# Attention loop of a two-layer megakernel: the transposes move into the PSUM rings of the scores, three banks read by VectorE and four read by ScalarE

## What is computed

```python
def _L1_attn_ref(x, Wqkv, bqkv, Wo, bo):     # 32 query heads, 8 key/value heads, head size 8
    qkv = jnp.einsum('bsd,df->bsf', x, Wqkv) + bqkv
    ...
    k = jnp.repeat(k, N_REP, axis=2)
    v = jnp.repeat(v, N_REP, axis=2)
    scores = jnp.einsum('bqhd,bkhd->bhqk', q, k) / np.sqrt(HEAD_DIM)
    attn = jax.nn.softmax(scores, axis=-1)
    out = jnp.einsum('bhqk,bkhd->bqhd', attn, v).reshape(bsz, seqlen, D_MODEL)
    return jnp.einsum('bsd,de->bse', out, Wo) + bo
```

## Time and profile before

| what | value |
|---|---|
| runs | 674.20, 677.84, 679.25 us; median 677.84 |
| the profiled execution, its own time | 674.86 us |
| span of its trace | 673.0 us |
| mean granted TensorE clock | 0.977 of full speed |
| attention loop in the trace | some 361 to 567 us |
| 13 "o" transposes of steps c = 12 to 60 | 398.57 to 535.13 us |

### The profile page before, as it was taken

The page is one execution under the profiler, slowest core; times in us unless marked ns, Lnnn a source line. Parts: engine busy times, 40 slices in busy tenths (PEclk is TensorE's granted clock), DMA queues, the critical chain, the costliest instruction groups (busy, mean ns, idle before and its releaser), DMA issues.

```text
span 673.0 us, 11796 instructions
## 1 busy us (share of the span) xinstructions
PE 617.5 (92%) x4298; PEld 408.7 (61%) x4298; DVE 400.7 (60%) x929; ACT 326.0 (48%) x645; POOL 213.5 (32%) x312
## 2 busy tenths in 40 slices
PE   3999999999999989799989899999999999979990
PEld 2887887887888775466566444444444446546660
DVE  4526605733751586333387979989899955633336
ACT  4523423432432324233326488888888885413322
POOL 5870651381082164523422121201010101421331
PEclk9999999999999999899979999999999999989995
DMA  6000200200199994314199991000000000031213
GB/s 218 33 1 33 95 1 32 93 1 1 68 265 278 77 270 138 96 39 135 50 310 333 282 118 3 1 2 1 2 1 2 1 2 1 25 99 44 80 56 125
DMA packets 69000, 57.40 MB, mean 85 GB/s; under 512 B 21520, under 2 KB 64400, under 8 KB 68944
## 3 DMA queue, kind: packets, MB, share of 16 engines
q1 hardware_dynamic: 66736, 50.60, 32.3%
q0 software_dynamic: 2208, 6.05, 2.5%
HBM read 30.78 MB, written 25.85 MB: 84 GB/s over the span
## 4 chain that ended last, share of the span: by engine, by line
PE 76%; DVE 7%; ACT 6%; DMA 4%; POOL 2%; issue 2%; another core or an unknown queue 1%; SPq 0%; ACTq 0%; POOLq 0%; DVEq 0%
PE psum L1604 9%; PE psum L303 9%; PE psum L1574 8%; PE psum L304 8%; PE psum L305 8%; PE psum L1289 8%; PE psum L1318 5%; PE psum L1560 4%; ACT pr L1473 3%; PE psum L1213 2%; DVE stat L666 2%; PE psum L1532 2%; PE psum L1199 1%; PE psum L1589 1%; PE psum L1206 1%
## 5 line engine op out<-in xcount | busy, mean ns | idle before, releaser
L1710 DVE TENSOR_REDUCE mx<-psum 128x1 f32<-128x512 f32 x256 | 158.7, 682 | 20.2 <-PE psum L1574 19.4
L1473 ACT ACTIVATE pr<-psum 128x512 f32<-128x512 f32 x256 | 138.8, 598 | 27.6 <-PE psum L1589 26.8
L1574 PE MATMUL psum<-kT,qT 32*128 32x512 f32 x256 | 78.5, 497 | 2.7 <-DVE mx L1710 1.6
L1604 PE MATMUL psum<-pr,vals 128*32 128x256 f32 x1024 | 78.9, 395 | 0.0
L1589 PE MATMUL psum<-qT,kT 32*128 32x512 f32 x256 | 66.5, 496 | 0.0
L1574 PEld LDWEIGHTS psum<-kT,qT 32*128 32x128 f32 x256 | 33.9, 182 | 47.2 <-issue 22.5
L1289 PE MATMUL psum<-w_gu,xgT 128*128 x120 | 57.5, 602 | 0.0
L624 POOL DMA_INDIRECT routed_y<-yr,xg x30 | 28.9, 962 | 84.3 <-DVE yr L876 83.7
L1514 POOL CAST mp<-mx 128x16 bf16<-128x16 f32 x16 | 3.2, 198 | 154.3 <-DVE mx L1710 154.3
L1046 ACT ACTIVATE sg<-psum,xg 128x256 f32<-128x256 f32 x30 | 14.2, 474 | 63.1 <-PE psum L1289 59.1
L867 DVE SCALAR_TENSOR_TENSOR h<-psum,xg,sg 128x256 f32<-128x256 f32 x30 | 14.5, 484 | 50.8 <-ACT sg L1046 50.8
(11 more groups left out here) (214 smaller groups left out, 1401.5 us busy)
## 6 DMA issues: line engine op xcount, KB each, us to landing
sorted_x<-zeros SPq DMA_DIRECT2D x2, 9088.0 KB, 41.7
w_gu<-in_L_ffn_gate_w SPq DMA_DIRECT2D x16, 256.0 KB, 6.3
w_gu<-in_L_ffn_up_w SPq DMA_DIRECT2D x16, 256.0 KB, 6.4
w_d<-in_L_ffn_down_w SPq DMA_DIRECT2D x16, 256.0 KB, 6.4
xg<-sorted_x SPq DMA_DIRECT2D x30, 129.0 KB, 2.2
wk_f<-in_L_attn_Wk SPq DMA_DIRECT2D x4, 512.0 KB, 5.2
wq_f<-in_L_attn_Wq SPq DMA_DIRECT2D x4, 512.0 KB, 5.9
wv_f<-in_L_attn_Wv SPq DMA_DIRECT2D x4, 512.0 KB, 3.6
```

The lines of the kernel that those rows point to most:

```text
L1473: nc.scalar.activation(pr[d % 3][:, j], s2_bank(d, j), ACT.Exp, scale=SCALE).then_inc(exp_ready, 1)
L1574: mm(s1_bank(c, j), qT1[n % 2][rows, t * P:(t + 1) * P], kT[n // GH][rows, :], start=True, stop=True).then_inc(s1_made, 1)
L1604: last = mm(ps[AV_BANK][j * VW:(j + 1) * VW, cols], vals[:, n // NKV * TB + kc, n % NKV // GH * GH + j, :], pr[d % 3][:, j, cols], start=( ...
L1710: v.tensor_reduce(mx[n % 2][:, t, j:j + 1], s1_bank(c, j), AX.X, ALU.max, negate=True).then_inc(max_read, 1)
```

## The change

The bank of a tile is no longer fixed by its kind. Two lists are written out ahead of the loop. FOR_DVE holds what VectorE reads, in the order in which TensorE makes it: the four `scores1` tiles of a step, and behind them an "o" transpose, for the steps that have one while c < 64; they take turns in banks 0, 1, 2. FOR_ACT holds what ScalarE reads: the `scores2` tiles with the "q1", "q2" and "k" transposes between the second and the third, and the last three "o" (n = 13 to 15, at c = 64, 68, 72); they take turns in banks 3, 4, 5, 7. Whatever it is, an item waits until the item three (four) places ahead in its list has been read (`wait_bank`).

In TensorE's list the "o" transpose moves from between the two halves of the scores to behind both, ahead of the two `weigh` halves. `turn_att` now waits for 13 outputs in place of 8, because banks 0 and 1 are shared with outputs; `keep_warm`'s dummy matmuls at the end use a spare bank. VectorE, ScalarE and GpSimd keep their lists of instructions; only banks change there.

```diff
-        RING = 3
+        DVE_BANKS, ACT_BANKS = (0, 1, 2), (3, 4, 5, 7)
...
+        LATE_O = (STEPS - 12) // TB
+        FOR_DVE, FOR_ACT = [], []
+        for c_ in range(END):
+            new = [x_ for x_ in turns_at(c_)]
+            if c_ < STEPS:
+                FOR_DVE += [("s1", c_ * GH + j) for j in range(GH)]
+                FOR_DVE += [x_ for x_ in new if x_[0] == "o"]
+            if c_ >= LAG:
+                S2 = [("s2", s2_no(c_ - LAG, j)) for j in HEADS2] if c_ < STEPS + LAG else []
+                FOR_ACT += S2[:2] + [x_ for x_ in new if x_[0] != "o"] + S2[2:]
+                FOR_ACT += [x_ for x_ in new if x_[0] == "o" and x_[1] >= LATE_O]
...
+        def wait_bank(pe, item):
+
+            ring, banks = (FOR_DVE, DVE_BANKS) if item in FOR_DVE else (FOR_ACT, ACT_BANKS)
+            at_ = ring.index(item) - len(banks)
+            if at_ < 0:
+                return
+            kind, n = ring[at_]
+            if kind == "s1":
+                pe.wait_ge(max_read, n + 1)
+            elif kind == "s2":
+                pe.wait_ge(exp_ready, n + 1)
+            else:
+                wait_read(pe, ring[at_])
...
             def turn(what):
                 n = TURNS.index(what)
-                if n >= 2:
+                if what in FOR_DVE or what in FOR_ACT:
+                    wait_bank(pe, what)
+                elif n >= 2:
                     wait_read(pe, TURNS[n - 1])
...
                 for j in (2 * i, 2 * i + 1):
-                    k = c * GH + j
-                    if k >= RING:
-                        pe.wait_ge(max_read, k - RING + 1)
+                    wait_bank(pe, ("s1", c * GH + j))
...
                 for what in turns_at(c):
-                    if what == ("o", NG - 1):
-                        keep_warm(2, 3)
-                    turn(what)
+                    if what[0] != "o":
+                        turn(what)
                 if c < STEPS:
                     scores1(c, 1)
...
+                for what in turns_at(c):
+                    if what[0] == "o":
+                        if what[1] == NG - 1:
+                            keep_warm(2, SPARE)
+                        turn(what)
                 if 0 <= d - 2 < STEPS:
                     if (d - 2) % TB == 0:
                         weigh(d - 2, 0)
```

More of the change, by code:

```diff
@@ L1360, in build @@
         QKV_AT = 3
-        RING = 3
+        DVE_BANKS, ACT_BANKS = (0, 1, 2), (3, 4, 5, 7)
         HEADS2 = (2, 3, 0, 1)
         AV_BANK, TURN_BANK = 6, 7
-        def s1_bank(c, j):
-            return ps[(c * GH + j) % RING]
         def s2_no(d, j):
             return d * GH + HEADS2.index(j)
-        def s2_bank(d, j):
-            return ps[RING + s2_no(d, j) % RING]
         def turns_at(c):
@@ L1396, in turn_no, with bank_no, s1_bank, s2_bank @@
             return TURNS.index(what) + 1
-        def turn_bank(n):
-            return ps[AV_BANK] if n == 0 else ps[TURN_BANK]
+        LATE_O = (STEPS - 12) // TB
[9 more added lines that the diff above has]
+                FOR_ACT += [x_ for x_ in new if x_[0] == "o" and x_[1] >= LATE_O]
+        SPARE = [i for i in ACT_BANKS if all(ACT_BANKS[FOR_ACT.index(("o", n)) % len(ACT_BANKS)] != i
+                                             for n in range(LATE_O, NG))][0]
+        def bank_no(item):
+            if item in FOR_DVE:
+                return DVE_BANKS[FOR_DVE.index(item) % len(DVE_BANKS)]
+            if item in FOR_ACT:
+                return ACT_BANKS[FOR_ACT.index(item) % len(ACT_BANKS)]
+            return AV_BANK if item == FIRST[0] else TURN_BANK
+        def s1_bank(c, j):
+            return ps[bank_no(("s1", c * GH + j))]
+        def s2_bank(d, j):
+            return ps[bank_no(("s2", s2_no(d, j)))]
+        def wait_bank(pe, item):
[10 more added lines that the diff above has]
+                wait_read(pe, ring[at_])
         def wait_read(eng, what):
@@ L1439, in copy_turn @@
                 dst = kT[n] if kind == "k" else (qT1 if kind == "q1" else qT2)[n % 2]
-                nc.scalar.activation(dst[:], turn_bank(TURNS.index(what)), ACT.Copy).then_inc(turn_copied, 1)
+                nc.scalar.activation(dst[:], ps[bank_no(what)], ACT.Copy).then_inc(turn_copied, 1)
             def hi_parts(b, t):
@@ L1541, in turn @@
                     pe.wait_ge(qkv_ready, TB)
-                into = turn_bank(n)
+                into = ps[bank_no(what)]
                 kind, i = what
@@ L1584, in scores2 @@
                 for j in HEADS2[2 * i:2 * i + 2]:
-                    k = s2_no(d, j)
-                    if k >= RING:
-                        pe.wait_ge(exp_ready, k - RING + 1)
+                    wait_bank(pe, ("s2", s2_no(d, j)))
                     rows = slice(j * HW, (j + 1) * HW)
@@ L1611, in turn_att @@
                 if t < TB:
-                    pe.wait_ge(att_ready, NKV)
+                    pe.wait_ge(att_ready, LATE_O)
                     pe.wait_ge(max_read, GH * STEPS)
@@ L1678, in pe_l1 @@
                     project(c - PROJ_AT - 1)
-            keep_warm(4, 3)
+            keep_warm(4, SPARE)
             for t in range(TB, NT):
@@ L1715, in outputs @@
                 dve.wait_ge(turned, turn_no(("o", n)))
-                o = ps[TURN_BANK].rearrange("p (t h w) -> p t h w", t=TB, h=GH)
+                o = ps[bank_no(("o", n))].rearrange("p (t h w) -> p t h w", t=TB, h=GH)
                 link(v.reciprocal(dn[:], o[:, :, :, HD]))
```

## The result

The changed kernel took 682.12 us in the median (eight runs, 677.79 to 685.19), the kernel before beside it 675.99 (eight runs, 673.73 to 679.25). The ratio is 1.009, with a 95% interval of 1.0062 to 1.0118: slower, by 0.6 to 1.2%. The forecast was 680.3, slower by 2.5 us. The profiled execution is the shortest of the eight, 677.79 us, 2.9 more than that of before.

The account below looks back on a forecast made before the run. The prediction took the loop to be bound by engines waiting for each other, none alone. Thirteen steps A at 0.23 us gave +3.0, less 0.5 behind c = 64: 677.84 + 2.5 = 680.3 us, range 675.0 to 685.0.

Parts of the forecast that it names:

- What bounds the loop: Attention loop: no engine alone sets the pace at 89 to 95% busy; how each waits for the others counts.
- Part 1, the output transpose: Step A, 13 times: the transpose behind all scores waits for VectorE's maxima, making the step 0.30 us longer.
- Part 2, the gain of 0.07 in step C: Step C: with four ScalarE banks the second `scores2` tile no longer waits for the exponential just ahead; 0.07 us gained.
- Part 3, behind c = 64: Loop's end: second pairs stop waiting for exponentials, the transpose at c = 68 waits for one; -0.5 us in all.
- The sum: Whole kernel: 3.0 us lost in the loop less 0.5 behind c = 64, +2.5 us.
- The rest of the program, put at no change: Work outside the loop, and the loop up to c = 11: order and banks that matter kept, no change.
- Rival 3, the clock: Step A: scores 0.6 us apart lower TensorE's clock, 1.2 us a fall; in all 13, 695.4 us; chance 0.07.
- The rule on emptied pipelines: VectorE's maxima would follow at 0.68 us, so the transpose starts later: +7.4 us more, 687.7; chance 1 in 100.

Follow-up runs that it names:

- E1: Kernel before, its banks kept, with only the output transpose moved behind all four scores; 683.37 us against 674.68, ratio 1.0128.
- E4: Changed kernel with the next group's queries' transpose (q1) moved two steps earlier, into step A between the score halves; 669.42 us against 674.68, ratio 0.991.

## Why the prediction came out as it did

- *What bounds the loop.* Right: no engine alone, but the path through step A. E1 and E4 show it from both sides, one making the loss larger by order alone, the other taking it away and more by using the waiting time.
- *Part 1, the output transpose.* Right in mechanism and nearly in size. A2, A3 and the transpose go out 0.6 apart; the transpose waits for A1's maximum. From `scores1` A2 to B0 the trace has 462.34 - 459.56 = 2.78, the working 469.15 - 466.37 = 2.78. VectorE's idle time ahead of B0 was forecast as 0.56 and is 0.49. Ahead of B2 the prediction gave no figure of its own beyond "0.5 to 0.6 us ahead of B0, and again ahead of B2", and it is 0.30. Ahead of C2 it was to be as before, 0.48, and is 0.47.
- *Part 2, the gain of 0.07 in step C.* Wrong. `scores2` in step C still stands 0.1 behind the `scores1` beside it (465.31 against 464.94 + 0.77 - 0.50 = 465.21), and C0 to C2 takes 466.89 - 464.94 = 1.95, as before. What holds it isn't the ring of three; what it is stays open. This is the term that makes the period 11.59 and not 11.54: over twelve periods, with the two longer ones, 140.12 against 136.56, +3.6 us where 12 x 0.23 = 2.8 was forecast.
- *Part 3, behind c = 64.* Right. The second pairs last 0.50 in place of 0.74, and at c = 68 the transpose waits for an exponential:

```profile
559.90 0.50 PE L1620 MATMUL psum<-qT,kT 32*128 32x512 f32 x2
...
566.61 0.66 PE L1595 MATMUL psum<-ident,oT 128*128 128x128 f32 x4 [0.73 <-ACT pr L1506]
567.20 1.07 PE L1635 MATMUL psum<-pr,vals 128*32 128x256 f32 x16
```

From the weighs of c = 64 to the last run of weighs the changed kernel takes 570.68 - 553.70 = 16.98, the one before 564.39 - 546.85 = 17.54: -0.56, forecast -0.5.
- *The sum.* +2.5 forecast, +3.3 measured from c = 12 on in the shortest execution. The 0.8 is the 0.07 of part 2, twelve times.
- *The rest of the program, put at no change.* Wrong in the traces, in both directions. In the pair of profiled executions it is +3.0 ahead of c = 12 and -3.2 behind the loop. That their times lie 2.9 apart, close to the 2.5, is therefore luck in part: two differences that the working had put at nothing nearly cancel.
- *Rival 3, the clock.* It was set up as all or nothing, 13 falls and 695 us, at 0.07. It happened in a small way: one fall in each of two traces out of four, at just the place named, at 1.56 and 1.51 us where 1.2 was worked out. In the mean of the four traces that is 0.8 us. The mean granted clock of the first eight executions goes with their times: 0.980 at 677.8 us, 0.972 and 0.973 at 680.3 to 680.9, 0.967 and 0.968 at 683.3 to 685.2. No trace of the changed kernel is of an execution with as low a clock as 0.968 (they have 0.976 to 0.980), so where the falls of the long ones lie wasn't seen.
- *The rule on emptied pipelines.* The Trainium skill, "VectorE: DVE Perf Modes", section "The DRAIN you can't avoid", says that the next operation doesn't start until the pipeline is empty, and adds in the same place that one that isn't held starts earlier. The trace of the changed kernel has ten maxima in 6.07 us, 0.60 each and not 0.68. That speaks against the first sentence as the prediction took it; it doesn't contradict the second, which the prediction left out.

The sign and the size of the loop's part came out because the working went through one period instance by instance and found the wait behind the one removed. The difference of the medians came out 3.6 us short (6.1 measured, 2.5 forecast): 0.8 of it is the loop's period, and 2.8 is not in that period. In the mean of the four traces 0.8 us is falls of the clock in steps A, to which the working gave one price for thirteen and none for one or two. The traced executions took 677.8 to 679.8 us, all under the median of 682.1, so how the remaining 2 us divide between the loop and the stages outside it stays open.

## What to carry to other kernels

When a wait is covered by moving an instruction behind other work, look at what that other work waits for: here 0.57 us of waiting for a copy became three bank waits in a row, and the moved transpose stood behind them all. A gap in a list that runs in order is better filled with something that is ready (an operand for the next group) than with the tiles that share the scarce buffer. Working out one period with each release written down gave the sign of the change, and the loss per period to within 0.05 us, before the kernel ran; the average busy times of 89 to 95% gave neither. And before a difference of medians is put down to the stage that was changed, cut the traces into stages and compare each: here the stages that nobody had touched differed by as much as the one that was.

## What the runs showed of the hardware

- The granted clock can fall inside a stretch in which TensorE shows as busy 97% of the time (141.17 of 145 us in the trace with the fall shown above): scores of 32 rows that go out 0.6 us apart count as busy in the trace and still came ahead of a fall to half speed. In most other steps A the same staircase came ahead of none.
- A higher busy share is not a faster loop. TensorE's busy time from 400 to 545 us rose from 138.2 to 141.2 us, in the trace without a fall too, while the loop got slower, because a pair that waits between its two matmuls is shown as one busy stretch.
- Executions of one program differ by 11.4 us (677.19 to 688.56 in the second timing of the changed kernel), nearly in step with the mean granted clock, 0.981 to 0.963.
- Falls of the clock also change in stages whose own work is the same: from the last `weigh` to the end of the span the traces take 105.2 to 108.9 us.
